# A five-layer graph network on one core: the sort's slots and columns summed by TensorE, and the relation passes in seven runs through four PSUM banks

## The reference

```python
def _rgcn_conv(x, src, dst, edge_type, inv_deg, basis, comp, root, bias):
    xs = x[src]
    c = comp[edge_type]
    m = c[:, 0:1] * (xs @ basis[0])
    for b in range(1, basis.shape[0]):
        m = m + c[:, b:b + 1] * (xs @ basis[b])
    agg = jax.ops.segment_sum(m * inv_deg[:, None], dst, num_segments=n_nodes)
    return agg + x @ root + bias
...
h = _rgcn_conv(x, src, dst, edge_type, inv_deg, basis1, comp1, root1, bias1)
h = jax.nn.relu(h)
return _rgcn_conv(h, src, dst, edge_type, inv_deg, basis2, comp2, root2, bias2)
```

## Time and profile before

| | us |
|---|---|
| median of 3 runs (lowest to highest) | 5314.03 (5310.81 to 5316.79) |
| profiled execution, time | 5313.37 |
| its span, first to last instruction | 5311.6 |
| busy in the span: TensorE, VectorE, ScalarE, GpSimd | 4640.2, 4125.2, 2967.5, 1156.1 |
| GpSimd's share of the sort: busy in 400 to 600 us | 150.74 of 200 |
| TensorE, VectorE, ScalarE busy in 400 to 600 us | 158.43, 149.39, 162.37 of 200 |

### The profile page before, as it was taken

How to read it: one execution, slowest core, us unless ns; L and a number is a source line. 1 busy time by engine, 2 the same in 40 slices (tenths; PEclk the granted TensorE clock), 3 DMA queues, 4 the chain that set the end, 5 groups by cost and what they waited for, 6 DMA issues and landing times.

```text
span 5311.6 us, 255849 instructions
## 1 busy us (share of the span) xinstructions
PE 4640.2 (87%) x101193; PEld 4003.4 (75%) x101193; DVE 4125.2 (78%) x6986; ACT 2967.5 (56%) x9065; POOL 1156.1 (22%) x1736
## 2 busy tenths in 40 slices
PE   1878778766999999599969999889999998999998
PEld 1666666646999999588869999867777776777776
DVE  8677777778999999888888899876666666666665
ACT  2878878741222222377753333366666666666665
POOL 2677777751111111000002222200000000000000
PEclk7989989977999999799989999999999999999999
DMA  1000000006877888300014444333333333333332
GB/s 49 2 1 1 1 1 1 1 16 188 253 255 253 253 254 253 119 3 0 0 39 123 120 121 121 95 97 89 91 88 90 90 87 91 90 90 91 90 90 76
DMA packets 305223, 501.39 MB, mean 94 GB/s; under 512 B 76919, under 2 KB 78455, under 8 KB 305127
## 3 DMA queue, kind: packets, MB, share of 16 engines
q1 hardware_dynamic: 303782, 499.39, 32.2%
q0 software_dynamic: 576, 0.52, 0.1%
q10 hardware_dynamic: 768, 0.16, 0.0%
HBM read 408.40 MB, written 91.57 MB: 94 GB/s over the span
## 4 chain that ended last, share of the span: by engine, by line
PE 50%; POOL 16%; issue 15%; DVE 10%; ACT 4%; POOLq 2%; DMA 1%; DVEq 0%; ACTq 0%; SPq 0%
PE PS L1501 18%; PE PS L1494 9%; PE PS L1297 7%; PE PS L1275 4%; PE PS L1277 4%; DVE arena L1815 4%; POOL arena L787 2%; ACT arena L1034 2%; PE PS L1548 2%; PE PS L1292 2%; PE PS L1531 1%; POOL arena L632 1%; POOL arena L640 1%; ACT arena L1046 1%; ACT arena L858 1%
## 5 line engine op out<-in xcount | busy, mean ns | idle before, releaser
L1815 DVE TENSOR_TENSOR arena<-iotab,arena 128x1024 bf16<-128x1024 bf16 (+3 forms) x1789 | 1735.4, 1000 | 466.3 <-PE PS L1501 389.9
L1034 ACT ACTIVATE arena<-PS 128x384 bf16<-128x384 f32 x2450 | 1067.0, 494 | 600.8 <-PE PS L1494 600.8
L1501 PE MATMUL PS<-arena 32*128 32x193 bf16 (+1 forms) x41552 | 1080.1, 243 | 5.2 <-DVEq L2454 1.9
L1501 PEld LDWEIGHTS PS<-arena 32*128 32x128 bf16 x41552 | 814.7, 92 | 194.5 <-issue 163.5
L858 ACT ACTIVATE arena<-PS,m 128x196 bf16<-128x196 f32 x1813 | 743.1, 429 | 189.8 <-PE PS L1143 185.0
L1494 PE MATMUL PS<-Hp,arena 128*128 128x192 bf16 (+1 forms) x4900 | 643.5, 249 | 90.7 <-DVE Hp L1661 34.7
L1494 PEld LDWEIGHTS PS<-Hp,arena 128*128 128x128 bf16 x4900 | 338.8, 99 | 302.4 <-issue 178.3
L1275 PE MATMUL PS<-Hp,arena 128*128 128x72 bf16 x7350 | 499.4, 198 | 42.8 <-DVE arena L2155 40.4
L1277 PE MATMUL PS<-arena 128*128 128x72 bf16 x7350 | 500.1, 198 | 0.0
L1150 PE MATMUL PS<-arena,tmp 128*128 128x262 bf16 x1813 | 487.4, 298 | 12.2 <-DVE ewB L1847 7.1
L1015 ACT ACTIVATE arena<-PS,ewB 128x64 f32<-128x64 f32 x1176 | 256.5, 329 | 417.8 <-PE PS L1337 417.8
(11 more groups left out here) (373 smaller groups left out, 8293.9 us busy)
## 6 DMA issues: line engine op xcount, KB each, us to landing
arena<-hots SPq DMA_DIRECT2D x735, 256.0 KB, 2.6
arena<-codes SPq DMA_DIRECT2D x245, 512.0 KB, 5.0
hots<-arena SPq DMA_DIRECT2D x245, 256.0 KB, 5.1
arena<-hots SPq DMA_DIRECT2D x147, 320.0 KB, 2.9
arena<-codes SPq DMA_DIRECT2D x49, 640.0 KB, 5.3
hots<-arena SPq DMA_DIRECT2D x49, 320.0 KB, 5.4
rows_h<-Hn SPq DMA_DIRECT2D x4, 1568.0 KB, 9.4
rows_l<-Y SPq DMA_DIRECT2D x1, 1764.0 KB, 10.0
```

What stands on the lines that cost most here:

```text
L1034: act.activation(RG[g % 2][:, 2 * i:2 * i + 2, 0:RW], ps[PAIR_BANK[q]][:, 0:2 * RW].rearrange("p (k c) -> p k c", k=2), ACT.Copy).then_inc ...
L1501: last = pe.matmul(ps[2 + q][:, b * SW:b * SW + SW - o], one_hot[32 * q:32 * q + 32, b * P:(b + 1) * P], rows_of[32 * q:32 * q + 32, 0:SW ...
L1815: return dve.tensor_tensor(to.rearrange("p k (n t) -> p k n t", t=4), iota_of[:, 0:n].rearrange("p (n t) -> p n t", t=4)[:, None, :, :] .t ...
```

## The change

**Sort.** GpSimd no longer works out slot and column. It makes five small vectors and two flags of the ranks (`own32`, `high`, `ovb`, `over`, with `w2c`, `wrel` and `tgc`). TensorE adds them up by nine matmuls instead of two, with scaled identities (`less32`, `plus32`, `times177`) and the triangle `place_b`, at step 8 rather than step 11. VectorE takes both results from bank 6: the column by a maximum, the slot by a minimum with the prefix sum, each written four times over. GpSimd waits only where it reads what it just wrote, and it now waits for VectorE (`k_oe`) at the start of the next block's `places`.

**Relation passes.** The 50 columns go in seven runs of 8, 6, 8, 8, 4, 8, 8. A run's pairs take banks 0, 1, 6, 7 in this order, so that TensorE gathers a whole run and then scatters a whole run. The one-hot matrices have four buffers instead of two, the gathered rows three. `transform` and `turn_sums` wait until banks 6 and 7 are copied, and gathers into them wait for the turned sums and the output taken. VectorE reads the sums of four banks by one `tensor_reduce`, and takes the output of two blocks before right behind.

```diff
-PAIR_BANK = (0, 1, 6, 0, 1, 6, 0, 1, 6, 0, 1, 6, 0, 1, 0, 1, 0, 1, 0, 1, 0, 1, 6, 0, 1)
+RS = (8, 6, 8, 8, 4, 8, 8)
+R0 = (0, 8, 14, 22, 30, 34, 42)
+NR = len(RS)
...
+SHORT = 4
+LONG_BANKS = (0, 1, 6, 7)
+OUT_TAKEN = R0[2] // 2 + 3
+PAIR_BANK = tuple(b for n in RS for b in LONG_BANKS[0:n // 2])
...
+TURNED = tuple(min(q for q in range(R0[SHORT + 1] // 2, NP) if PAIR_BANK[q] == b) for b in LONG_BANKS[2:])
+HOT_BUFFER = (0, 1, 2, 0, 1, 2, 3)
+ROW_BUFFER = (0, 1, 0, 1, 0, 1, 2)
...
+                if not is_zero(dx):
+                    pool.wait_ge(k_oe, dx)
+                    pool.wait_ge(k_col, dx)
+                    pool.sem_inc(s_held, 1)
+                made(pool.tensor_tensor(w2c, w2[:, bass.ds(c, NJ)], wbase[:, bass.ds(dx, 1)].to_broadcast((P, NJ)), ALU.add))
+                made(pool.tensor_tensor(wrel, w2[:, bass.ds(c, NJ)], wown[:, bass.ds(dx, 1)].to_broadcast((P, NJ)), ALU.add))
+                made(pool.tensor_copy(tgc, tg32[:, bass.ds(c, NJ)]))
+                settled(True)
+                made(pool.tensor_scalar(own32, wrel, 0.0, 32.0, ALU.is_equal, ALU.mult))
...
+                pool.tensor_copy(rec4[par], rec3[:, bass.ds(c, NJ), :][:, :, :, None].to_broadcast((P, NJ, REC, 4)))
                 pool.wait_ge(k_rank, dx * NJ + NJ + 4)
...
+                settled()
+                made(pool.tensor_tensor(high, rank[par], own32, ALU.subtract))
+                settled(True)
+                made(pool.tensor_scalar(ovb, high, 32.0, None, ALU.is_ge))
+                pool.tensor_scalar(over, rank[par], 32.0, None, ALU.is_ge).then_inc(k_ov, 1)
+                settled()
+                pool.tensor_tensor(XO[par][:, :, 0], ovb, w2c, ALU.mult)
+                pool.tensor_tensor(XO[par][:, :, 1], ovb, tgc, ALU.mult).then_inc(k_col, 1)
...
-                pool.wait_ge(k_oe, dx + 1)
...
                     if ranks:
                         if j == 0 and not is_zero(dx):
-                            act.wait_ge(k_free, dx)
+                            act.wait_ge(k_ovp, dx)
...
+                        n = scatters_before(g, ROW_BUFFER)
+                        for i in range(RS[g] // 2):
+                            q = R0[g] // 2 + i
+                            act.wait_ge(r_gath, dx * NP + (o * WINDOWS * NP + q + 1))
+                            if i == 0 and not (is_zero(dx) and o == 0 and n < 1):
+                                act.wait_ge(r_scat, dx * NR + (o * NNR + n))
...
             def overflow(dx):
+
...
-                pe.matmul(ps[6][:, 0:NJ], before_b[:, :], ovb, start=True, stop=True)
-                pe.matmul(ps[6][:, NJ:2 * NJ], onesb[:, :], ovb, start=True, stop=True).then_inc(k_ovp, 1)
+                slot_at, before_at, total_at, col_at = (ps[6][:, n * NJ:(n + 1) * NJ] for n in range(4))
+                pe.matmul(slot_at, identb[:, :], high, start=True, stop=False)
+                pe.matmul(slot_at, identb[:, :], own32, start=False, stop=False)
+                pe.matmul(slot_at, identb[:, :], tgc, start=False, stop=False)
+                pe.matmul(slot_at, less32[:, :], over, start=False, stop=False)
+                pe.matmul(slot_at, plus32[:, :], ovb, start=False, stop=True)
+                pe.matmul(before_at, place_b[:, :], ovb, start=True, stop=True)
+                pe.matmul(total_at, onesb[:, :], ovb, start=True, stop=True)
+                pe.matmul(col_at, times177[:, :], over, start=True, stop=False)
+                pe.matmul(col_at, identb[:, :], ovb, start=False, stop=True).then_inc(k_ovp, 1)
 
...
-                    if t == 11 and placed:
+                    if t == 8 and placed:
                         overflow(dx)
...
+                        q = R0[g] // 2 + i
+                        hot = max(h for h in range(NG) if G0[h] <= 2 * q)
+                        if 2 * q == G0[hot]:
+                            pe.wait_ge(f_hot[hot], dx * 16 + ((o + 1) * WINDOWS + 1) * 16)
                         if not (is_zero(dx) and pairs_to_wait(q) < 1 and o == 0):
                             pe.wait_ge(r_ev, dx * NP + (o * WINDOWS * NP + pairs_to_wait(q)))
...
+                        if q == OUT_TAKEN and not (first or second):
+                            pe.wait_ge(z_done, dx + o * WINDOWS)
+                        if q in TURNED and not (is_zero(dx) and o == 0):
+                            pe.wait_ge(z_tc, dx * 2 + (o * WINDOWS * 2 - 1 + TURNED.index(q)))
...
+                            last = scatter_typed(RO[HOT_BUFFER[g]][:, k, :], RG[ROW_BUFFER[g]][:, k, :],
+                                                 g == 0 and k == 0, False)
...
+                        for g in range(NR):
+                            if g == 0 and not (first or second):
+                                pe.wait_ge(r_ev, dx * NP + (o * WINDOWS * NP + R0[1] // 2))
+                                transform(dx - 2)
+                            if g < NR - 1:
+                                for i in range(RS[g + 1] // 2):
+                                    gather_rows(dx, g + 1, i, first, second)
+                            elif not last:
+                                for i in range(RS[0] // 2):
+                                    gather_rows(dx + 1, 0, i)
+                            if g == SHORT - 1 and not first:
+                                pe.wait_ge(r_ev, dx * NP + (o * WINDOWS * NP + R0[SHORT] // 2))
+                                turn_sums(dx - 1, 0)
+                                turn_sums(dx - 1, 1)
+                            for i in range(RS[g] // 2):
+                                scatter_rows(dx, g, i)
                         scatter_few(dx)
...
+            def overflow(dx, par):
...
+                slot_at, before_at, total_at, col_at = (ps[6][:, n * NJ:(n + 1) * NJ] for n in range(4))
                 dve.wait_ge(k_ovp, dx + 1)
-                klink(dve.tensor_tensor_scan(oscan, ps[6][:, NJ:2 * NJ], zero37, 0.0, ALU.add, ALU.add))
-                klink(dve.tensor_tensor(oe, oscan, ps[6][:, 0:NJ], ALU.add))
-                klink(dve.tensor_tensor(oe, oe, ps[6][:, NJ:2 * NJ], ALU.subtract))
-                dve.sem_inc(k_oe, 1)
+                dve.tensor_tensor_scan(oscan[:, 1:NJ], total_at[:, 0:NJ - 1], zero37[:, 1:NJ], FAR,
+                                       ALU.add, ALU.add).then_inc(k_step, 1)
+                at[1] += 1
+                dve.tensor_tensor(colv4[par], fours(col_at), fours(w2c), ALU.max)
+                dve.wait_ge(k_step, at[0] + at[1])
+                klink(dve.tensor_tensor(oe, oscan, before_at, ALU.add))
+                dve.tensor_tensor(slot4[par], fours(oe), fours(slot_at), ALU.min).then_inc(k_oe, 1)
 
             def columns_hot(dx, par):
-                dve.wait_ge(k_col, dx + 1)
+                dve.wait_ge(k_oe, dx + 1)
                 dve.wait_ge(k_exp, dx * NB + NB)
-                klink(compare(OCOL, iotab, colv4[par]))
+                klink(compare(OCOL, iotab[:, P:2 * P], colv4[par]))
...
+                if b == 0:
+                    dve.wait_ge(k_col, dx + 1)
...
-                    dve.wait_ge(r_scat, dx * NG + (o * NN + g + 1))
-                    compare(RO[g % 2][:, 0:GS[g], :], iotab1, r_cdw[:, G0[g]:G0[g] + GS[g], :]).then_inc(r_oh, 1)
+                    if not (is_zero(dx) and o == 0 and n < 1):
+                        dve.wait_ge(r_scat, dx * NR + (o * NNR + n))
+                    compare(RO[HOT_BUFFER[g]][:, 0:RS[g], :], iotab1, r_cdw[:, R0[g]:R0[g] + RS[g], :]).then_inc(r_oh, 1)
...
                         dve.tensor_scalar(per.rearrange("p (q b) -> p q b", b=2), met, 1.0, None, ALU.max)
-                    for q in range(4):
-                        last = dve.tensor_reduce(Zs[:, 2 * q:2 * q + 2, :],
-                                                 ps[2 + q][:, 0:2 * SW].rearrange("p (b x) -> p b x", b=2)[:, :, 0:RW]
-                                                 .rearrange("p b (a c) -> p b c a", a=PARTS), AX.X, ALU.add)
-                    flink(last)
+                    sums = PS[:, 2 * 512:6 * 512].rearrange("p (q x) -> p q x", q=4)[:, :, 0:2 * SW] \
+                        .rearrange("p q (b x) -> p q b x", b=2)[:, :, :, 0:RW].rearrange("p q b (a c) -> p q b c a", a=PARTS)
+                    flink(dve.tensor_reduce(Zs.rearrange("p (q b) c -> p q b c", b=2), sums, AX.X, ALU.add))
...
-                    for g in range(NG):
+                    for g in range(NR):
                         if g == 0 and not first:
                             take_sums(dx - 1)
-                        if g < NG - 1:
-                            one_hots(dx, g + 1)
+                            if not second:
+                                take_out(dx - 2)
+                        if g < NR - 2:
+                            one_hots(dx, g + 2)
                         elif not last:
-                            one_hots(dx + 1, 0)
-                        if g == 2 and not (first or second):
-                            take_out(dx - 2)
```

(1 more changed line is left out.)

171 lines of the change are left out of this document (56 added, 115 removed).

## The result

The changed kernel takes 4963.4 us (median of 4 runs, 4960.2 to 4966.0) where the kernel before, run beside it on the same chip, takes 5313.6 us: a ratio of 0.934, 95% interval 0.932 to 0.936. That is 350 us less.

What follows compares the result with a forecast made beforehand. It took GpSimd's serial instructions to bound the sort and TensorE the relation passes. From 5313.4 us it took 164 for the sort and 152 for the relation passes and added 1 for preparation: 4998 us, range 4940 to 5090.

Steps and rivals of the forecast that it cites:

- The first step: Sort: GpSimd's 28 instructions in series are the round, 20.69 us a block; TensorE's wait for it goes, VectorE's with it.
- the count of switches: Relation passes: twelve stretches each of gathers and scatters become seven, saving 5 x (0.10 + 0.12) = 1.1 us a block.
- the new wait at `z_free`: Relation passes: TensorE waits 0.6 us for VectorE in front of each block's first scatter.
- the round of 17.2 us: Sort: a block takes 17.2 us instead of 20.69, saving 164 us in 47 blocks.
- TensorE's round of 17.1 us: Sort: TensorE's whole round without GpSimd in its way, including a 0.81 us wait for ScalarE and some slow columns.
- VectorE's floor: Sort: VectorE's 16.2 us of work plus 0.4 for the new operations limits a block to 16.6 us.
- Rival 3: Sort limited only by VectorE's work (16.6 us), relation passes saving 1.75 us a block: 4950 us; chance 0.1.
- GpSimd's slack: Sort: three GpSimd operations take about 1.2 us, so the flags are ready 1.9 us before TensorE asks at step 8.
- Rival 1: Sort: GpSimd's operations stretch beside busy VectorE, flags come 1.1 us after step 8, block 18.3 us, total 5050; chance 0.15.
- the turned sums' wait: Relation passes: a run of 64 scatters covers the wait for the turned sums, freeing 0.42 us a block.
- The +1 us: Preparation: four more constants add 1 us.
- The point that would have been wrong in kind: Sort: TensorE's column steps getting slower than 0.40 us, since all of the 17.2 us round rests on them.

Runs made afterwards that it cites:

- rank_bank6: The changed kernel with the ranks of column 36 in PSUM bank 6 instead of bank 0: 4935.2 us, ratio 0.9287.
- dve_extra: The changed kernel with one more VectorE compare a sort block, over 15 of the 37 columns, into a tile nobody reads: 4966.9 us, ratio 0.9344.
- flags_step5: The changed kernel with TensorE asking for the overflow flags at column step 5 of a sort block instead of 8: 4977.0 us, ratio 0.9359.
- Run 6: Not an experiment: the last of a relation block's seven column runs, counted from 0, with 8 columns; its gathers take 0.88 us to the next scatter, not 0.77.
- pool_extra: The changed kernel with one more GpSimd compare of 37 columns, into a row nobody reads, in front of the one for `ovb`: 4974.4 us, ratio 0.9355.
- all_three: The changed kernel with column 36's ranks in bank 6, two code copies made by GpSimd, and two gathers moved before a block's first scatters: 4948.6 us, ratio 0.9300.

## Why the prediction was right, and where it was off

**The mechanisms.** The first step, that GpSimd's series was the round of the sort and that VectorE's wait would go with it, held: the 64.6 us for GpSimd in the earlier trace rows became 7.5 on the weight loads and none that the matmuls show. So did the count of switches and their price of 0.22 us a pair, the new wait at `z_free` (0.5 us in pass 1 and 0.3 in pass 2 for 0.6 forecast), the one reduce (1.75 us, as taken), and that nothing else waits for long. VectorE is at 94.5% for "over 90%". GpSimd is at 53% for "under half".

**The sort, 164 us forecast, 204 to 206 measured.** The term that was mis-sized is the round of 17.2 us; it is 16.45. Two things went wrong.
- TensorE's round of 17.1 us, 602.19 to 619.30, had the slow columns in it. The prediction said that they go with the wait that causes them, and then did not take them off. In the trace of before, four column steps behind the wait take 0.71 us each, where they take 0.40 now, 1.2 us more for the four; the granted clock is 0.50 from 602 to 605 us, right behind the wait, and 1.00 in the sort's blocks now. Taken off, the 17.1 would have been 15.9. Even that is no work of TensorE alone: its steps of 0.39 are at ScalarE's pace, and the turn's 0.81 stands in it. Two of the four, in the trace of before, start to start:

```profile
602.37 0.37 PE L1142 MATMUL PS<-agg,own_b 128*128 128x196 bf16 x1
...
603.08 0.37 PE L1142 MATMUL PS<-agg,own_b 128*128 128x196 bf16 x1
...
603.78 0.37 PE L1142 MATMUL PS<-agg,own_b 128*128 128x196 bf16 x1
```

- VectorE's floor was 16.6, 16.2 of work and 0.4 added. VectorE stands 0.6 us in each round of 16.45, so its work is 15.85 at most, and with 0.55 us more the round is still 16.47. The prediction read its 16.2 from one of the longest rounds, 21.33 where the mean is 20.69. The compare over 37 columns that took 1.30 us in the earlier trace rows (and 1.16 in every other block) now takes 1.15 in all; why isn't shown. What the new operations add is small too: the four take 0.79 us where the three took 0.69.

What the sum lacked is a term for ScalarE. In the table above its own work is 15.7 us of a block; the turn at bank 0 adds 0.56 and TensorE's long steps 0.22, and that is the whole 16.5. The turn is a wait that stands in the earlier trace rows (0.81 us for ScalarE) and in the earlier trace rows, and the prediction counted it as a part of TensorE's round and not as something that could hold the round by itself. `rank_bank6` shows what it was worth: 0.56 us a block. Rival 3, "VectorE's work is the only limit", had the time nearest (4950), but by a limit that isn't there: half a microsecond more of VectorE's work (`dve_extra`) costs nothing. So the 35 us between forecast and result are nearly all the sort's, 42 us more than forecast, with the relation passes 7 us below theirs; no large errors cancel.

**GpSimd's slack.** The estimate that three operations take 1.2 us came from the earlier trace rows, where VectorE and TensorE stood still. They take 3.0 us with their waits. Rival 1 had this right, and had 1.25 us for each, where only one takes so long; the flags come at step 8, not 1.1 us behind it. What rival 1 lacked is the second half: even a wait of 1.0 us (`flags_step5`) costs only 0.2 us a block, since the ranks in four banks lie between. The Trainium skill, SBUF — State Buffer, section SBUF: two separate sides, has VectorE and GpSimd lock each other out of a shared port pair for a whole instruction; for VectorE that holds when it runs in a two-port mode, or reads two inputs from SBUF while GpSimd reads there too, as its compares and products do here. The trace agrees that GpSimd's small operations stretch from 0.26 to 1.25 us while VectorE runs its operations of 1.24 us, and end 0.1 to 0.2 us after them. No run takes VectorE's work away to test it. The rule was the better guide to GpSimd's time than rows from a quiet stretch; it was no guide to the total.

**The relation passes, 152 us forecast, 145 measured.** The sum of 1.55 us a block came out at 1.48 in the mean. A pair of stretches is 0.22 us, as taken, so their 1.1 held. Run 6's gathers wait 0.1 us for a bank, the tight place that the prediction named with "none to spare". The rest, about 0.5 us, is what the turned sums' wait had to give with the end of the block; 0.42 was taken for it, and no run separates the two. The four reduces would have cost 0.2 us of it, inside the bounds of 1.75 and 1.94.

**The +1 us** of preparation: L1170 and L1155 both start first at 149.0, so it was nothing that can be seen. The 3.5 us of the weighted sums were not foreseen. They go with the clock at the beginning of that stage, and not with the change.

**The point that would have been wrong in kind,** column steps slower than 0.40 us, did not come: they are 0.40, which is ScalarE's pace.

## What to carry to other kernels

When a long wait is removed from a ring of engines, take the slow columns behind it off the round as well, and then look for the shortest wait that is left in every round: with three engines above 90% the bound may be no engine but a turn, here two consecutive users of one bank, which an idle bank undoes for 27 us. A busy share, even of all the time, doesn't show that an engine has nothing left, since operations overlap in it; the distances between its starts do. A small difference in a stage that the edit doesn't touch should be looked for in the other kernels' traces before the edit is named as its cause. A delay on an engine that runs ahead of the next one is worth what is left when the queue between them is empty, a fifth here; price it at the engine behind. And a small operation's row from a quiet stretch is no price for it beside a busy neighbour, while its duration is no price for leaving it out: that is the distance between two starts.

## What the runs showed of the hardware

- An operation of GpSimd on 128x37 elements takes 0.26 us while VectorE waits, and 0.72 to 1.25 beside its long ones; a second one right behind the 1.25 takes 0.72, after and in `pool_extra` alike, and a third 0.30. The long ones end 0.1 to 0.2 us after an operation of VectorE ends.
- Delays of ScalarE of 0.05 to 0.1 us between two ranks stand in no list of waits, and make up 0.2 us a block (0.47 in `all_three`). Only the starts of its operations show them.
- A change between gathers of 128 rows and scatters of 32 costs TensorE 0.11 us, either way; its weight loads pause 0.16 us at it.
- Small ScalarE copies out of PSUM overlap: 0.25 us long, 0.10 us apart.
- One VectorE reduce over four PSUM banks with five levels of access takes 1.75 us for 1536 elements; four take 1.94. So reaching over the banks costs nothing that can be seen; no run reads the same elements without the other strides.
- One stage with the same code begins with the granted clock at 0.87 to 0.91 over its first 20 us in seven of the fourteen traces and at 0.67 to 0.69 in six, and lasts 658 us in the former and 662 in the latter; in one it begins at 1.00 and lasts 656.
